# A field-interaction network on one core: one more pair of tiles split into high and low parts, lows moved between VectorE and GpSimd, high parts copied to PSUM

## What is computed

```python
for idx, (W, b) in enumerate(params):          # W: (39, fk, 128), fk = 39, 64, 64
    z = jnp.einsum('bhd,bkd,hks->bsd', x0, xk, W) + b[None, :, None]
    z = jax.nn.relu(z)
    if idx != n_layers - 1:
        half = z.shape[1] // 2
        xk = z[:, :half, :]
        direct.append(z[:, half:, :])
    else:
        direct.append(z)
logit = jnp.sum(jnp.concatenate(direct, axis=1), axis=-1)
h = relu([logit, dense_ctx] @ W_top1 + b_top1); h = relu(h @ W_top2 + b_top2); y = h @ W_top3
```

## Time and profile before

| what | value |
|---|---|
| median of 3 runs | 2543.64 us (2540.9 to 2547.57) |
| profiled execution, its own time | 2545.02 us |
| its span, first to last instruction | 2543.1 us |
| first matmul of layer 1 in the first chunk | 100.40 us |
| last matmul of layer 2 in the last chunk starts | 2469.19 us |
| granted TensorE clock, mean | 0.995 |

### The profile page before, as it was taken

One profiled execution on the slowest core, in us unless ns is written; L12 is line 12 of the kernel. 1 busy time (PEld: TensorE's weight loads), 2 busy tenths in 40 slices (PEclk: granted clock), 3 DMA queues, 4 the chain that ended last, 5 costly groups with the idle time before them and its releaser, 6 DMA issues.

```text
span 2543.1 us, 25999 instructions
## 1 busy us (share of the span) xinstructions
PE 2432.8 (96%) x7712; PEld 1423.5 (56%) x7712; DVE 2268.7 (89%) x1356; ACT 1175.5 (46%) x1414; POOL 1557.9 (61%) x1029
## 2 busy tenths in 40 slices
PE   0599999999999999999999999999999999999999
PEld 0265555556555555555555565555556555555553
DVE  0599999999999999999999999999999999999960
ACT  0244444445454444545444444444444444445442
POOL 6476667667666766766676666667666766743240
PEclk9899999999999999999999999999999999999999
DMA  2986777777677777867777776787777677766610
GB/s 69 246 211 180 199 207 202 180 217 214 176 198 205 207 178 215 209 182 197 209 206 177 217 206 190 190 211 210 178 207 205 200 184 213 207 182 194 195 30 0
DMA packets 262712, 477.02 MB, mean 188 GB/s; under 512 B 19500, under 2 KB 37788, under 8 KB 262614
## 3 DMA queue, kind: packets, MB, share of 16 engines
q1 hardware_dynamic: 141766, 271.07, 38.9%
q10 hardware_dynamic: 100480, 200.29, 28.5%
q0 software_dynamic: 20448, 5.45, 1.4%
HBM read 468.99 MB, written 7.74 MB: 187 GB/s over the span
## 4 chain that ended last, share of the span: by engine, by line
PE 73%; POOL 10%; DVE 6%; issue 4%; DMA 4%; ACT 2%; SPq 0%; POOLq 0%; DVEq 0%; ACTq 0%
PE z L693 37%; PE z L716 33%; POOL emb L352 5%; DVE prod L418 4%; POOL pair_lo L211 4%; DMA emb<-in_tbl,idx 3%; PE xk L775 1%; PE z L775 1%; DMA x_pairs<-x_transposed 1%; ACT pair_hi L532 1%; POOL half_parts L207 1%; DVE pair_lo L211 1%; PE turned L674 1%; DVE logit L448 1%; ACT xk L542 0%
## 5 line engine op out<-in xcount | busy, mean ns | idle before, releaser
L418 DVE TENSOR_TENSOR prod<-x_pairs,xk 128x2048 f32<-128x2048 f32 x640 | 1436.4, 2284 | 75.2 <-PE z L716 46.9
L693 PE MATMUL z<-prod,w_plain 128*128 128x512 f32 (+2 forms) x2944 | 1383.1, 594 | 40.5 <-DVE prod L418 40.5
L532 ACT CAST pair_hi<-prod 128x1024 fp32r<-128x1024 f32 x703 | 735.4, 1046 | 1085.2 <-PE z L716 793.6
L211 POOL TENSOR_TENSOR pair_lo<-prod,pair_hi 128x1024 fp32r<-128x1024 f32 x320 | 764.1, 2388 | 638.3 <-ACT pair_hi L532 621.7
L693 PEld LDWEIGHTS z<-prod,w_plain 128*128 128x128 f32 (+2 forms) x2944 | 555.4, 189 | 474.1 <-issue 394.9
L352 POOL DMA_INDIRECT emb<-in_tbl,idx x624 | 701.3, 1124 | 184.0 <-issue 173.7
L716 PE MATMUL z<-pair_hi,w_lo 128*128 128x512 f32 (+1 forms) x1408 | 786.6, 559 | 2.3 <-DVE pair_lo L211 1.7
L716 PE MATMUL z<-pair_hi,w_hi 128*128 128x512 f32 (+1 forms) x1408 | 555.7, 395 | 0.0
L716 PE MATMUL z<-pair_lo,w_hi 128*128 128x512 f32 (+1 forms) x1408 | 555.1, 394 | 0.0
L211 DVE TENSOR_TENSOR pair_lo<-prod,pair_hi 128x1024 fp32r<-128x1024 f32 (+1 forms) x384 | 468.5, 1220 | 48.7 <-ACT pair_hi L532 48.7
L716 PEld LDWEIGHTS z<-pair_hi,w_lo 128*128 128x128 f32 (+1 forms) x1408 | 265.2, 188 | 297.2 <-POOL pair_lo L211 135.8
(11 more groups left out here) (50 smaller groups left out, 566.5 us busy)
## 6 DMA issues: line engine op xcount, KB each, us to landing
x_pairs<-x_transposed SPq DMA_DIRECT2D x64, 2432.0 KB, 16.9
x_pairs<-x_transposed ACTq DMA_DIRECT2D x64, 2432.0 KB, 19.3
x_diag<-x_transposed SPq DMA_DIRECT2D x128, 546.0 KB
x_diag<-x_transposed ACTq DMA_DIRECT2D x64, 546.0 KB
x_pairs<-x_transposed SPq DMA_DIRECT2D x64, 256.0 KB, 20.4
emb<-in_tbl,idx POOLq DMA_INDIRECT x624, 6.3
x_diag<-x_transposed SPq DMA_DIRECT2D x128, 78.0 KB
x_transposed<-stage SPq DMA_DIRECT2D x32, 156.0 KB
```

Source lines behind the costliest of these rows:

```text
L211: engine.tensor_tensor(pair_lo[0:rows, pair % PAIR_RING], held[0:rows, at:at + 2, :], pair_hi[0:rows, pair % PAIR_RING].bitcast(F32), ALU. ...
L418: nc.vector.tensor_tensor(prod[0:rows, pos % RING, 0:n, :], a, xk.unsqueeze(1).broadcast_to([rows, n, N]), ALU.mult).then_inc(prod_ready, 1)
L532: nc.scalar.copy(pair_hi[0:rows, pair % PAIR_RING], held[:, at:at + 2, :]).then_inc(hi_ready, 1)
L693: ins = nc.tensor.matmul(z[n][:], w, held[0:rows, i, :], start=(k == 0 and i == plain[0]), stop=(k == last_slot and not here and i == plai ...
```

## The change

- `SPLITS` names the engine of each low. Layer 2 gets a second pair in slot 3 (places 2 and 3), so all four tiles of this slot are split. There are now 12 pairs in a chunk instead of 11. GpSimd has the lows of layer 1's slots 0 and 1 and all of layer 2 but the new pair: 7 pairs and a half tile. VectorE has layer 0, layer 1's slots 2 to 4 with the half tile, and the new pair: 5 pairs and a half tile.
- For VectorE's lows in layers 1 and 2 ScalarE writes the rounded pair a second time, into PSUM (`hi_copy`, two banks that the transposes use too; the half tile into `direct01`, which moves to PSUM), and VectorE subtracts this copy.
- `hi_parts` and `lo_parts` have places for three pairs; `PLACES` gives each pair its place, and a rounding waits for the pair three before.
- `xk0` shares the bank of `xk2`: the hand-on of xk2 also waits for layer 0's last product.
- TensorE's layer 0 waits for both of its slots, starts with the second, and frees both at its end. The transposes come after layer 0. ScalarE's stage copies come after `direct_0` of layer 2 in chunk 1.
- `logit01` and `logit2` keep 512 columns; a window of 128 is stored to DRAM once per group and loaded again for the top stage (4 more loads).
- 20 gathers ahead instead of 30; GpSimd gathers between its lows of layer 1 and of layer 2.

```diff
-SPLITS = {0: [(0, 0, 2)],
-          1: [(0, 0, 2), (1, 0, 2), (2, 0, 2), (2, 3, 1), (3, 0, 2), (4, 0, 2)],
-          2: [(0, 0, 2), (1, 0, 2), (2, 0, 2), (2, 3, 1), (3, 0, 2), (4, 0, 2)]}
-EARLY = {1: 4, 2: 4}
+V, G = "VectorE", "GpSimd"
+SPLITS = {0: [(0, 0, 2, V)],
+          1: [(0, 0, 2, G), (1, 0, 2, G), (2, 0, 2, V), (2, 3, 1, V), (3, 0, 2, V), (4, 0, 2, V)],
+          2: [(0, 0, 2, G), (1, 0, 2, G), (2, 0, 2, G), (2, 3, 1, G), (3, 0, 2, G), (3, 2, 2, V),
+              (4, 0, 2, G)]}
+EARLY = {1: 5, 2: 4}
...
-GATHERS_AHEAD = 30
-GATHERS_AT = [range(30, F), range(0, 10), range(10, 20), range(20, 30)]
-PAIR_RING = 2
+GATHERS_AHEAD = 20
+GATHERS_AT = [range(20, 30), range(30, F), range(0, 10), range(10, 20)]
+PARTS = 6
+PLACES, tile = {}, 0
+for n in (1, 0, 2):
+    PLACES[n] = []
+    for _, _, m, _ in SPLITS[n]:
+        PLACES[n].append(tile % PARTS)
+        tile += m if m > 1 else 0
...
-        turned = [ps("turned0"), ps("turned1")]
-        xk0 = ps("xk0")
+        hi_copy = ctx.enter_context(nc.psum_tensor("hi_copy", [P, 2, N], F32))
+        turned = [hi_copy[:, 0, :], hi_copy[:, 1, :]]
+        direct01 = ps("direct01")
         xk1, xk2 = ps("xk1"), ps("xk2")
+        xk0 = xk2
...
+            if m == 1:
+                hi = direct01[0:HALF] if copy else half_parts[0:HALF].bitcast(F32)
+                engine.tensor_tensor(half_parts[0:HALF], held[0:HALF, at, :], hi,
+                                     ALU.subtract).then_inc(done, 1)
+            else:
+                hi = (hi_copy[0:rows, 0:m, :] if copy else
+                      hi_parts[0:rows, place:place + m, :].bitcast(F32))
+                engine.tensor_tensor(lo_parts[0:rows, place:place + m, :], held[0:rows, at:at + m, :],
+                                     hi, ALU.subtract).then_inc(done, 1)
...
 GpSimd, group
+                    done = lows_of(1, chunk, 0, split, pos)
+                    if c == 2 and len(fields_at[c]):
+                        start_group(bt + 2, False)
+                    gather(fields_at[c])
...
+                    lows_of(2, chunk, done, split, pos)
+                    if c == 1 and len(fields_at[2]):
+                        pool.wait_ge(gathered, 16 * (bt + 2) * F)
+                        pool.sem_inc(waits_held, 1)
                         load_indices(bt + 2)
...
 VectorE, layer 2 of a chunk
                     for k in range(SLX):
                         product(slot + k, pos + k, copies[:, FIRST_TILE[k]:FIRST_TILE[k] + QUAD, :],
                                 xk2[:])
                         if k == 1:
-                            sum01(chunk)
+                            sum01(bt, c)
+                        split = subtract(late, split)
+                        late = splits_of(2, pos, k, chunk)
+                    subtract(late, split)
...
 ScalarE, round_splits
-                        act.wait_ge(slot_free, RING + held_by[-PAIR_RING] + 1)
-                        nc.scalar.copy(pair_hi[0:rows, pair % PAIR_RING], held[:, at:at + 2, :]
+                        act.wait_ge(slot_free, RING + used_by[place + m - 1] + 1)
+                        nc.scalar.copy(hi_parts[0:rows, place:place + m, :], held[:, at:at + m, :]
                                        ).then_inc(hi_ready, 1)
+                    if n and who == V:
+                        copies = [s for s in SPLITS[n][0:i] if s[3] == V]
+                        if m == 1:
+                            nc.scalar.copy(direct01[0:HALF].bitcast(F32R), held[0:HALF, at, :]
+                                           ).then_inc(hi_copied, 1)
+                        else:
+                            if any(s[2] == m for s in copies):
+                                last = max(j for j, s in enumerate(copies) if s[2] == m)
+                                act.wait_ge(lo_ready[V],
+                                            len(SPLITS[0]) + chunk * LOWS_C[V] + last + 1)
+                            nc.scalar.copy(hi_copy[:, 0:m, :].bitcast(F32R), held[:, at:at + m, :]
+                                           ).then_inc(hi_copied, 1)
...
 ScalarE, group
+                        round_splits(0, slice(0, None), slot, pos, used_by, chunk)
+                        act.wait_ge(prod_ready, slot + SL0)
                     hand_on(1, xk2, b1_sb, slot)
...
-                    if c == 1 and not last:
-                        fill_stage(bt + 1)
...
                         hand_on(0, xk1, b0_sb, slot)
-                        act.wait_ge(summed01, chunk + 1)
+                        act.wait_ge(summed01, chunk + 2)
                         direct_0()
+                        if c == 1 and not last:
+                            fill_stage(bt + 1)
+                            act.wait_ge(stage_ready, 2 * (bt + 2))
+                        round_splits(2, slice(EARLY[2], None), slot, pos, used_by, chunk)
...
 TensorE
+            def layer0(slot, pos, lows):
+                pe.wait_ge(prod_ready, slot + SL0)
+                held = prod[:, (pos + SL0 - 1) % RING]
+                t = L0_FIRST[SL0 - 1]
+                for i in range(T0 - t):
+                    plain_part(0, t, i, held, i == 0, False)
+                for i in range(QUAD):
+                    if L0_FIRST[0] + i not in SPLIT_TILES[0]:
+                        plain_part(0, L0_FIRST[0], i, prod[:, pos % RING], False, False)
+                for i, (s, place) in enumerate(zip(SPLITS[0], PLACES[0])):
+                    ins = split_part(0, 0, s, place, lows, False, i == len(SPLITS[0]) - 1)
+                    lows[s[3]] = lows[s[3]] + 1
+                ins.then_inc(slot_free, SL0)
...
+                    if not (last and c == CHUNKS - 1):
+                        layer0(slot, pos, lows)
+                        slot, pos = slot + SL0, pos + SL0
                     if c == 1 and not last:
                         transpose_group(bt + 1)
```

More of the change, by code:

```diff
@@ L78 @@
 NB = 512
-assert CB < NB < B and len(SPLITS[0]) == 1
+assert CB < NB < B and all(k == 0 for k, _, _, _ in SPLITS[0])
 def top_order():
@@ L439, in subtract @@
-            def subtract(item, split, pair):
-                n, pos, at, m = item
-                dve.wait_ge(hi_ready, split + 1)
-                low_part(nc.vector, n, pos, at, m, pair)
-                return split + 1, pair + (m == 2)
-            def sum01(chunk):
-                dve.wait_ge(direct01_ready, 2 * chunk + 2)
-                nc.vector.tensor_reduce(logit01[:, bass.ds(chunk * CB, CB)],
+            def subtract(late, split):
+                for n, pos, copy, place, k, at, m, who in late:
+                    if who == V:
+                        if copy is None:
+                            dve.wait_ge(hi_ready, split + 1)
+                        else:
+                            dve.wait_ge(hi_copied, copy + 1)
+                        low_part(nc.vector, n, pos + k, at, m, place, copy is not None, lo_ready[V])
+                    split += 1
+                return split
@@ new lines, in splits_of, with products @@
+            def splits_of(n, pos, slot, chunk):
+                copies, here = lows(1, V) if n == 2 else 0, []
+                for s, place in zip(SPLITS[n], PLACES[n]):
+                    copy = chunk * COPIES_C + copies if n else None
+                    copies += s[3] == V
+                    if s[0] == slot:
+                        here.append((n, pos, copy, place, *s))
+                return here
+            def products(n, copies, xk, slot, pos, late, split, chunk):
+                first_tile, rows, tiles = (FIRST_TILE, P, TX) if n else (L0_FIRST, R0, T0)
+                for k, first in enumerate(first_tile):
+                    product(slot + k, pos + k, copies[0:rows, first:min(first + QUAD, tiles), :],
+                            xk[0:rows])
+                    split = subtract(late, split)
+                    late = splits_of(n, pos, k, chunk)
+                return late, split
@@ L456, in sum2 @@
                                         z[2][:].rearrange("p (d b) -> p b d", b=CB),
                                         AXIS.X, ALU.add).then_inc(summed2, 1)
-            def layer(n, copies, xk, slot, pos):
-                return [(n, k, copies, xk, slot + k, pos + k) for k in range(SLX if n else SL0)]
-            products(layer(0, x0_diag, xk0, 0, 0), 0, 0, 0)
+            dve.wait_ge(xk0_ready, 1)
+            late, split = products(0, x0_diag, xk0, 0, 0, [], 0, 0)
+            subtract(late, split)
@@ L601, in group @@
             def group(bt, last):
[L602 removed]
                 before = SL0 + bt * CHUNKS * SLC
[L605 removed]
+                used_by = {place + i: before - SLX + k for (k, _, m, _), place
+                           in zip(SPLITS[2], PLACES[2]) if m > 1 for i in range(m)}
                 for c in range(CHUNKS):
@@ L689, in layer @@
                     pe.wait_ge(prod_ready, slot + k + 1)
                     for i in plain:
```

(13 more changed lines are left out.)

258 lines of the change are left out of this document (132 added, 126 removed).

## The result

The changed kernel takes 2616.22 us (median of 4 runs, 2612.19 to 2619.59) against 2545.26 us for the kernel before (4 runs, 2540.9 to 2547.57). The ratio is 1.0274, with a 95% interval of 1.026 to 1.0288. 2603 was forecast, with a range of 2520 to 2650.

A forecast was written before the change was run, and what follows sets the result against it. TensorE was taken as the bound, with GpSimd's chain of lows in layer 2 just touching it. 47 ordinary chunks x 1.04 and 15 with transposes x 0.68 gave +59 us on 2545.0: 2604, stated as 2603; range 2520 to 2650.

The forecast's parts named there:

- The deciding step: Layer 2's slot 3: without plain tiles TensorE waits 2.0 us per chunk for GpSimd's low; period +1.04 us.
- E: The end of layer 1 in a chunk, from which the prediction counts times; 1266.60 in the kernel before.
- the loop: Layer 1's end, xk2, two products, sum, third product, rounding, GpSimd's lows, slots 3 and 4, layer 1: 37.71 us.
- The sum from PSUM: Sum over direct01 before layer 2's slot 2 product: 687 ns from PSUM against 1059 from SBUF, 0.37 us less.
- the copy into PSUM: Five more ScalarE copies per chunk, 4.8 us, four of 1.05 us each; VectorE waits some 2 us at slot 3.
- The slower rival: VectorE or ScalarE becomes late in layer 1: 0.3 to 1 us more per chunk, 2622 to 2667 us; chance 0.18.
- Transposes: Behind layer 0, covered by TensorE's wait; stage copies before slot 3's rounding make such chunks 38.64 us, +0.68.
- the term put at nothing: Logit windows, DMAs through DRAM, 20 gathers ahead instead of 30, head and tail: nothing, 0 to 3 us.
- the lock between VectorE and GpSimd: VectorE instructions with two SBUF inputs and GpSimd SBUF reads exclude each other; no gain expected, no overlap in layer 2.

The follow-up runs named there:

- f3_vfirst: Changed kernel with VectorE's pair first in layer 2's slot 3, both pairs rounded before xk1's hand-on, indices and stage copies early: 2524.12 us, ratio 0.9922.
- f2_eleven: Changed kernel without the second pair in layer 2's slot 3 (11 pairs), with indices and stage copies early: 2517.61 us, ratio 0.9896.
- f1_stage_early: Changed kernel with chunk 1's two stage copies moved between the roundings of layer 2's slots 1 and 2: 2590.43 us.
- e4_sum_sbuf: Changed kernel with the sum over direct01 reading SBUF again instead of PSUM: 2645.78 us.
- e5_lows_sbuf: Changed kernel without the PSUM copies of the high parts, so VectorE's lows of layers 1 and 2 read SBUF: 2696.79 us.
- e1_eleven: Changed kernel without the second pair in layer 2's slot 3 (11 pairs), all else as changed: 2675.23 us, ratio 1.0512.
- h1_eleven_sbuf: f2_eleven without the PSUM copies of the high parts, so VectorE's lows of layer 1 read SBUF: 2575.6 us.

## Why the prediction was right, and what it missed

*The deciding step held, and not by luck.* The edit that takes 0.31 us of work from slot 3 takes away its plain tiles as well. Forecast: GpSimd's low done at E+16.50, TensorE on it at E+16.62, a period of 37.71. Measured with E = 1303.06: E+16.37, E+16.53 (1319.82 less the 0.233 of one instruction, less E), period 37.65. f3_vfirst and f2_eleven show it from two sides, against f1_stage_early: something to run in front of the low is worth 66 us, the pair itself gone 73. The wait lies partly elsewhere than forecast: 1.57 us at slot 3 and 0.30 at slot 0 (1311.00 less 0.233 is 1310.77, against 1308.76 + 1.71 = 1310.47), where the kernel before had some 0.1; the loop does not care where. In the view of waits TensorE itself waits 102.2 us for GpSimd's lows, where about 125 were forecast for TensorE or its weight loads at slot 3.

*The loop was right.* The sum from PSUM takes 683 ns (687 forecast) and counts in full (e4_sum_sbuf).

*VectorE and ScalarE were off the loop.* The low from PSUM takes 1210 ns (1.22 forecast), the copy into PSUM 1012. VectorE waits 2.3 us for the copy (2 forecast); hand-on of xk2 is released by TensorE, never by layer 0's products. The slower rival did not occur.

*Transposes.* Chunk 1: 38.58 (38.64 forecast), by the stage copies, as said, and f1_stage_early confirms it. The mean of before was 37.82, not the 37.96 of the one chunk that I took: 2 us in all.

*What was missed* is the term put at nothing, "20 gathers ahead" and the DMAs. Index load and stage copies were moved next to each other, and neither was followed down its queue: SyncE's stores and loads stand behind the stage copies, and GpSimd's gathers behind the indices. That is 15 x 0.86 = 13 us in chunks 2, as much as lies between 2603 and 2616. Smaller things cancel: ordinary chunks are 3 us shorter in all than forecast, and head, top stage and first chunk together are longer by about as much. TensorE's clock, for which the prediction has no term, takes part in that: 5 us more of the first chunk ran at half clock. The prediction had asked what ScalarE's work delays on ScalarE, and not what waits for its result in another queue.

*Where the argument was weaker than its result.* I dismissed the lock between VectorE and GpSimd because GpSimd's lows of layer 2 did not overlap with VectorE's, and the gathers because they are not on the loop. Both were true of the kernel before. In the changed kernel GpSimd has lows in layer 1 and gathers with less slack, and only the copies, from which the prediction expected nothing, kept the lock away: without them the time is 81 us more. The Trainium skill ("SBUF — State Buffer", Who interferes with whom) gives the rule for two engines' lows, and e5_lows_sbuf agrees (1.21 to 1.84 us on one side, 2.4 to 3.2 on the other). It also says there, as inferred, that such a VectorE instruction takes only the read side, which the writing of descriptors does not need; yet here the gathers beside it take 1.73 and 2.50 us. Whether it is their descriptors or their indices, which they read from SBUF, that are held up, no run shows.

## What to carry to other kernels

Before splitting, moving or removing work on the busiest engine, ask what it was covering: the plain tiles that stood in front of a late low were worth 2 us of patience for 0.31 us of work. Close the loop by hand (who releases whom until it comes round) and price an edit only where it lies on it; everything else, here the shares of the lows and five copies a chunk, is worth nothing or less. Ask of work off the loop how much time it has left: the gathers cost nothing until they had none. When an instruction is moved, follow its result into every in-order queue that waits for it, DMA queues first.

## What the runs showed of the hardware

- A strided sum over 512 columns takes VectorE 1059 ns from SBUF and 683 to 687 ns from PSUM.
- A 19.5 KB load took 2.7 us to land at the median before and 10.6 us when issued among some 6.4 MB of other loads; a 546 KB load issued 2.7 us after a 2432 KB one on another queue reached its user some 21 us later (e1_eleven).
- An indirect DMA's issue on GpSimd takes 0.94 to 1.0 us beside a VectorE product or a subtraction with one input in PSUM, and 1.7 to 2.5 us beside subtractions with both inputs in SBUF (h1_eleven_sbuf).
- TensorE's granted clock fell to 0.50 for 10.2 us in chunks where it had stood for 8 us (e1_eleven), and for 3.4 us in eight chunks of e4_sum_sbuf and 14 of e5_lows_sbuf; split instructions then start 0.43 us apart instead of 0.233.
- In two of fourteen kernels TensorE's semaphore updates were seen up to 2.8 us after the matmul that carries them.
